# Two 16-head attention layers and the spectral layer between them, run as one pipeline of 16 units

## The reference

```python
x = x + tanh(g_xattn[0]) * one_head_attention(layernorm(x), ctx, mask)       # L0
x = x + tanh(g_ffn[0])   * experts_top_k(layernorm(x)) + shared expert
x = x + tanh(g_xattn[1]) * attention_16_heads(layernorm(x), ctx, bias, mask) # L1
x = x + tanh(g_ffn[1])   * real(ifft(fft(layernorm(x)) @ w)) + bias          # spectral, one 256 x 256 matrix
x = x + tanh(g_xattn[2]) * attention_16_heads(layernorm(x), ctx, mask)       # L2
x = x + tanh(g_ffn[2])   * ternary_mlp(layernorm(x))                         # 256 -> 1024 -> 256
x = x + tanh(g_xattn[3]) * one_head_attention(layernorm(x), ctx)             # L3
x = x + tanh(g_ffn[3])   * experts_top_1(layernorm(x))
```

## Time and profile before

| | us |
|---|---|
| median of 3 runs | 1054.77 (1049.65 to 1055.72) |
| profiled execution, its own time | 1053.23 |
| span of that execution, first to last instruction | 1051.4 |
| TensorE busy | 871.2 (83%) |
| VectorE busy | 445.3 (42%) |
| ScalarE busy | 359.1 (34%) |
| L1, spectral and L2 (from the last product of `spectral_matrix` to the last of L2) | 367.1 to 717.3 |

### The profile page before, as it was taken

The page is one execution under the profiler, slowest core; times in us unless marked ns, Lnnn a source line. Parts: engine busy times, 40 slices in busy tenths (PEclk is TensorE's granted clock), DMA queues, the critical chain, the costliest instruction groups (busy, mean ns, idle before and its releaser), DMA issues. The chain is left out here.

```text
span 1051.4 us, 15194 instructions
## 1 busy us (share of the span) xinstructions
PE 871.2 (83%) x5758; PEld 659.2 (63%) x5758; DVE 445.3 (42%) x1209; ACT 359.1 (34%) x731; POOL 201.4 (19%) x202
## 2 busy tenths in 40 slices
PE   4897999998888968898766799974679788379996
PEld 3774666677777845666554566642456576368885
DVE  1675544301222146654274665534766467400000
ACT  1432222121221225554311455442667543012221
POOL 0127100012344200000010000000345412501222
PEclk8996999998999969999976999996889999589999
DMA  6033600017554370000000000000000000234551
GB/s 202 21 121 121 244 10 11 22 41 264 167 184 118 61 280 1 1 2 2 1 1 0 1 2 1 2 1 1 0 1 1 1 29 34 95 110 157 176 180 18
DMA packets 33871, 70.54 MB, mean 67 GB/s; under 512 B 9219, under 2 KB 23947, under 8 KB 28940
## 3 DMA queue, kind: packets, MB, share of 16 engines
q1 hardware_dynamic: 27081, 60.18, 16.1%
q0 software_dynamic: 6144, 8.31, 4.2%
q10 hardware_dynamic: 578, 1.13, 0.3%
HBM read 54.98 MB, written 14.80 MB: 66 GB/s over the span
## 5 line engine op out<-in xcount | busy, mean ns | idle before, releaser
L1201 ACT ACTIVATE arena<-banks 128x512 f32<-128x512 f32 (+4 forms) x159 | 92.4, 599 | 286.9 <-PE banks L1063 54.9
L592 PE MATMUL banks<-arena 32*128 32x240 f32 (+6 forms) x1808 | 163.9, 381 | 19.2 <-DVE small L1882 14.8
L592 PE MATMUL banks<-ffw,arena 128*128 128x256 f32 (+2 forms) x640 | 126.9, 357 | 15.2 <-DVE x L1976 14.8
L592 PEld LDWEIGHTS banks<-arena 32*128 32x128 f32 (+5 forms) x1808 | 102.8, 165 | 53.1 <-issue 28.8
L592 PEld LDWEIGHTS banks<-ffw,arena 128*128 128x128 f16 (+1 forms) x640 | 87.3, 140 | 47.1 <-issue 23.4
L592 PE MATMUL banks<-arena,ew 128*128 128x256 f32 x512 | 115.1, 384 | 1.4 <-ACT arena L1201 1.4
L592 PE MATMUL banks<-ew,arena 128*128 128x256 f32 x512 | 115.6, 385 | 0.0
L592 PEld LDWEIGHTS banks<-arena,ew 128*128 128x128 f32 x512 | 98.4, 193 | 15.7 <-ACT arena L1201 2.1
L592 PEld LDWEIGHTS banks<-ew,arena 128*128 128x128 f32 x512 | 98.1, 194 | 13.2
L1882 DVE TENSOR_REDUCE small<-banks 128x16 f32<-128x1920 f32 x32 | 69.1, 2158 | 24.2 <-PE banks L592 23.8
L1380 ACT ACTIVATE arena<-banks,mcol 120x2048 f32<-120x2048 f32 x32 | 63.2, 1975 | 23.8 <-PE banks L592 23.8
(11 more groups left out here) (233 smaller groups left out, 1240.7 us busy)
## 6 DMA issues: line engine op xcount, KB each, us to landing
ew<-in_w SPq DMA_DIRECT2D x32, 1024.0 KB
xrow<-arena SPq DMA_DIRECT2D x1, 2064.0 KB, 21.5
arena<-xrow SPq DMA_DIRECT2D x8, 258.0 KB, 4.2
zrow<-arena SPq DMA_DIRECT2D x8, 256.0 KB, 2.2
ffw<-in_shared SPq DMA_DIRECT2D x2, 1024.0 KB, 7.0
acc<-x SPq DMA_DIRECT2D x4, 512.0 KB, 2.9
ffw<-in_tern SPq DMA_DIRECT2D x2, 1024.0 KB
out<-x SPq DMA_DIRECT2D x8, 256.0 KB, 2.0
```

Source lines behind the costliest of these rows:

```text
L592: return pe.matmul(o, l, r, start=a, stop=b)
L1201: return nc.scalar.activation(o, i_, ACT.Copy)
```

## The change

`multi_head(1)`, the spectral rounds and `multi_head(2)` become one function `stream()` on each engine, with units v = 0 to 15: units 0 to 7 are the batches in L1, 8 to 15 the same batches in L2. It runs steps s = 0 to 17. The spectral layer of batch j is put into step j+4, so eight steps (4 to 11, `free` in the code) hold it: on TensorE `spectral_turn(s-4)` takes the place of `turn_z(s+1)`, which moves behind `turned_scores(s-1,0)`; `queries(s+1)` moves behind `scores(s,1)`; `spectral(s-4)` and then `keys(s+1)` come behind `attend(s-1,0)`. The first works in bank 6, the second in bank 7. On ScalarE `take_z` moves behind the first `exps` and `take_back` behind `take_keys`. VectorE gets the spectral layer's statistics and norm one step ahead (steps 3 to 10) and its addition in steps 4 to 11, with buffers of their own (`zS`, `zST`, `veS`, `rstdS`). Three barriers go, those after the experts, L1 and the spectral layer; what is left is numbered anew. In place of the first, VectorE waits for `M_ps`, ScalarE for the experts' last result on VectorE, and SyncE for GpSimd's `later` before it writes the blank rows. The first unit's parts come in another order: keys, values, then the transposed rows and queries.

```diff
@@ SyncE
-            phase_end(sp, 1)
+            sp.wait_ge(su["later"], 7)
             sp.dma_start(xrow[0:T, :].rearrange("(t p) n -> p t n", p=P), bcast(blank, 1, NT)).then_inc(ex["blank"], 16)
@@ GpSimd
+                rstd_of(0)
+                rstd_of(1)
+                for s in range(UN):
+                    if s + 2 < UN:
+                        rstd_of(s + 2)
+                    if 3 <= s < NB + 3:
+                        g.wait_ge(f1["var"], s - 2)
+                        g.tensor_tensor(rstdS, veS, mhalf[:, 0:2], ALU.pow).then_inc(f1["rstd"], 1)
@@ TensorE
-            phase_end(pe, 1)
...
+                def turn_z(v):
+                    pe.wait_ge(q["z"], v + 1)
+                    pe.wait_ge(q["V_sb"], max(v, 1))
+                    if 3 <= v - 2 < NB + 3:
+                        pe.wait_ge(f1["zT_sb"], v - 4)
...
+                def turn_back(v):
...
+                    if 2 <= v < NB + 2:
+                        pe.wait_ge(f1["x"], v - 1)
...
+                def spectral_turn(j):
+                    pe.wait_ge(f1["z"], j + 1)
+                    pe.wait_ge(q["V_sb"], j + 5)
+                    o = psum[6].rearrange("p (k n) -> p k n", k=KC)
+                    for c in range(KC):
+                        for t in range(TB):
+                            m = pe.transpose(o[:, c, t * P:(t + 1) * P], zS[:, t, c * P:(c + 1) * P], ident[:, :])
+                    m.then_inc(f1["zT_ps"], 1)
+
+                def spectral(j):
+                    pe.wait_ge(f1["zT_sb"], j + 1)
+                    pe.wait_ge(q["mT_sb"], j + 4)
+                    for t in range(TB):
+                        for c in range(KC):
+                            m = mm(psum[7][:, t * D:(t + 1) * D], zST[:, c, t * P:(t + 1) * P], Mf[:, c, :],
+                                   c == 0, c == KC - 1)
+                    m.then_inc(f1["y_ps"], 1)
...
-                for part in (turn_z, queries, keys, values):
-                    part(0)
-                for s in range(NB + 2):
+                for part in (keys, values, turn_z):
+                    part(0)
+                queries(0)
+                for s in range(UN + 2):
+                    free = 4 <= s < NB + 4
                     if now:
                         scores(s, 0)
                     if old:
                         turn_max(s - 1)
-                    if new:
+                    if free:
+                        spectral_turn(s - 4)
+                    elif new:
                         turn_z(s + 1)
                     if past:
                         attend(s - 2, 1)
                     if old:
                         turned_scores(s - 1, 0)
-                    if new:
+                    if free:
+                        turn_z(s + 1)
+                    elif new:
                         queries(s + 1)
                     if past:
                         turn_O(s - 2)
                     if now:
                         scores(s, 1)
-                    if new:
+                    if free:
+                        queries(s + 1)
+                    elif new:
                         keys(s + 1)
                     if old:
                         attend(s - 1, 0)
+                    if free:
+                        spectral(s - 4)
+                        keys(s + 1)
                     if past:
                         turn_back(s - 2)
@@ ScalarE
+                act.wait_ge(ex["y_sb"], E)
+                for part in (take_keys, take_z, take_queries):
                     part(0)
...
                     if old:
                         exps(s - 1, 0)
+                    if free:
+                        take_z(s + 1)
                     if new:
                         take_queries(s + 1)
-                    if past:
+                    if past and not free:
                         take_back(s - 2)
                     if new:
                         take_keys(s + 1)
+                    if past and free:
+                        take_back(s - 2)
                     if old:
                         exps(s - 1, 1)
@@ VectorE
+                v.wait_ge(su["M_ps"], 1)
+                V.memset(Vx[:, :, :, HD:], 1.0)
                 take_values(0)
+                v.wait_ge(load["x0"], 32)
+                for n in range(2):
+                    norm_batch(n)
+                    norm_batch_end(n)
+                for s in range(UN + 2):
...
+                    if 3 <= s < NB + 3:
+                        spectral_stats(s - 3)
                     if s >= 2:
                         normalize(s - 2)
-                    if s < NB:
+                    if s < UN:
                         maxima(s, 1)
+                    if 4 <= s < NB + 4:
+                        add_spectral(s - 4)
-                    if s + 2 < NB:
+                    if s + 2 < UN:
                         norm_batch_end(s + 2)
+                    if 3 <= s < NB + 3:
+                        spectral_norm(s - 3)
```

More of the change, by code:

```diff
@@ L979, in keys, with values @@
                     m.then_inc(q["K_ps"], 1)
-                def values(k):
-                    pe.wait_ge(q["K_sb"], k0 + k + 1)
+                def values(v):
+                    L, k = layer(v)
+                    pe.wait_ge(q["K_sb"], v + 1)
                     for c in range(KC):
@@ L1065, in turn_back, with output @@
                     m.then_inc(q["oT_ps"], 1)
-                def output(k):
-                    pe.wait_ge(q["oT_sb"], k0 + k + 1)
+                def output(v):
+                    L, k = layer(v)
+                    pe.wait_ge(q["oT_sb"], v + 1)
                     for t in range(TB):
@@ L1201, in copy @@
                 return nc.scalar.activation(o, i_, ACT.Copy)
-            def take_z(q, i, u, banks=MISC):
-                act.wait_ge(q["zT_ps"], i * 2 + u + 1)
-                copy(zT[:, u], banks[u][:, :].rearrange("p (k n) -> p k n", k=KC)).then_inc(q["zT_sb"], 1)
             def take_weights(a, bank):
@@ L1387, in take_O, with take_back, take_spectral @@
                     copy(OP.rearrange("p g n -> p (g n)"), OW).then_inc(q["O_sb"], 1)
-                def take_back(k):
-                    act.wait_ge(q["oT_ps"], k0 + k + 1)
-                    if k >= 1:
-                        act.wait_ge(q["y_ps"], k0 + k)
+                def take_back(v):
+                    act.wait_ge(q["oT_ps"], v + 1)
+                    if v >= 1:
+                        act.wait_ge(q["y_ps"], v)
                     copy(OT2, psum[7].rearrange("p (k n) -> p k n", k=KC)).then_inc(q["oT_sb"], 1)
-                for part in (take_z, take_queries, take_keys):
+                def take_spectral(j):
+                    act.wait_ge(f1["zT_ps"], j + 1)
+                    copy(zST, psum[6].rearrange("p (k n) -> p k n", k=KC)).then_inc(f1["zT_sb"], 1)
@@ L1396, in multi_head @@
+                act.wait_ge(ex["y_sb"], E)
+                for part in (take_keys, take_z, take_queries):
                     part(0)
-                for s in range(NB + 2):
-                    new, old, past = s + 1 < NB, 1 <= s <= NB, 2 <= s
+                for s in range(UN + 2):
+                    new, old, past = s + 1 < UN, 1 <= s <= UN, 2 <= s
+                    free = 4 <= s < NB + 4
                     if old:
                         take_max(s - 1)
-                    if new:
+                    if free:
+                        take_spectral(s - 4)
+                    elif new:
@@ new lines, in spectral_norm @@
+                def spectral_norm(j):
+                    v.wait_ge(f1["rstd"], j + 1)
+                    if j >= 1:
+                        v.wait_ge(f1["zT_ps"], j)
+                    for t in range(TB):
+                        m = V.tensor_scalar(zS[:, t, :], x[:, 2 * j + t, :], mv[:, 2 + t, 0:1], rstdS[:, t:t + 1],
+                                            ALU.subtract, ALU.mult)
+                    m.then_inc(f1["z"], 1)
+                    v.drain()
+                    xt = x[:, 2 * j:2 * j + 2, :]
+                    V.tensor_tensor(xt, xt, bcast(rows[:, ROWS.index("f1"), :], 1, TB), ALU.add)
```

348 lines of the change are left out of this document (152 added, 196 removed).

## The result

The changed kernel takes 1010.55 us (median of 4 runs, 1007.92 to 1010.74), before 1055.07 in the same comparison; the ratio is 0.957, 95% interval 0.954 to 0.960. A second set of five runs of it gave 1010.51. The forecast was 1009.0, in a range of 999 to 1023.

What follows compares the result with a forecast made beforehand. The prediction took TensorE as busiest (83%), with the loss in filling and emptying the pipeline twice and the serial layer between. 109.28 - 49.1 - 18.0 + 2.0 = 44.2 us off 1053.2 gave 1009.0, range 999 to 1023.

Steps and rivals of the forecast that it cites:

- The seam: Between L1 and L2: 109.28 us go, three more full steps cost 49.1, net 60.2 less before the spectral work.
- The spectral work: Eight free steps: each 2.25 us longer than a full step, 18.6 in all; together 18.0 us more.
- the new wait for the exponentials: TensorE in a free step, before the second scores: stands 0.64 us because the queries no longer cover the exponentials.
- the wait of 0.77 before the values: TensorE in a free step: this wait goes, since ScalarE copies the keys ahead of `take_back`.
- the addition in bank 7: VectorE's spectral addition ahead of `turn_back` in a free step: ends about T+8.8, covered by the keys with 0.2 us spare.
- The start: From the spectral matrix to the first scores: keys and values first bring scores 2.0 us earlier, no clock gain taken.
- The pause before the transposes: TensorE in the start: stands some 3.7 us just ahead of the transposes, 4.65 before.
- Hand-overs bare: Rival: waits for copies in banks 6 and 7 of free steps lose 13 us, giving 1022; chance 0.14.
- Waits filled up: Rival: free steps of 17.26 and full clock at the start, 994 at the least, about 1000 if half; chance 0.10.
- the low bound of 17.26: Free step's length in us if neither the new wait nor the two old ones remained: 14.88 + 2.38.
- Seam: Rival: L1 empties and L2 fills as before, without the spectral stage; 22.1 us at worst, 1031; chance 0.03.
- The clock: Rival: TensorE's clock falls in free steps, 14.2 us more each, 1123 for all eight; chance 0.02.

Runs made afterwards that it cites:

- experiment 3: Changed kernel with ScalarE's old order in the free steps, the copy for the output ahead of the copy of the keys: 1013.78 us, ratio 0.962.
- experiment 4: Changed kernel with VectorE's spectral addition moved behind the two norms, just ahead of the values' addition: 1013.88 us, ratio 0.961.
- experiment 2: Changed kernel with the barrier after the experts put back and the first unit's parts in the old order: 1010.42 us, ratio 0.959.
- the control: The changed kernel run once more, unaltered: 1010.51 us, ratio 0.958.
- experiment 5: Changed kernel with the spectral product ahead of the second scores: 1001.29 us; or in halves, ahead of the first turned and the second scores: 997.03 us.

## Why the prediction was right

**The seam.** Forecast: 109.28 us go, 49.1 come. Measured: three more full steps in 49.10, steps 6 to 9 as long as their neighbours (18.54), so unit 8 waits for nothing that its neighbours don't. The pair without the spectral layer prices seam and start at 28.7 where the rows gave 29.2: 27.2 for the seam (22.1 for emptying and filling, 5.1 for the barrier and the first norms) and 2 for the start.

**The spectral work.** Forecast 18.6 a free step, measured 18.54; 8 x 2.25 = 18.0, measured 148.35 - 8 x 16.37 = 17.4. By its parts: the new wait for the exponentials 0.64, measured 0.60; the wait of 0.77 before the values gone, as ScalarE's order was the reason (experiment 3 brings it back to the hundredth); the addition in bank 7 hidden with 0.2 to spare, measured 0.15, and experiment 4 shows what stands behind that margin; VectorE ready 0.3 ahead of the values, measured 0.29.

**The start.** Forecast 13.84 from the spectral matrix to the first scores, measured 13.66, without the clock's gain, as taken. The pause before the transposes, put at 3.7, was 3.32. In the median the barrier and the start are not to be seen, in the traces they are (experiment 2).

**The sum.** The touched stretch came out 45.9 shorter in the trace, up to the ternary layer's first transposes, against 44.2 up to L2's last output. The difference is 0.6 in the eight steps, 0.2 in the start, 0.2 in steps 0 and 1, some 0.5 in the emptying, whose clock was 0.95 instead of 0.92, and 0.3 behind L2's last output. The part up to the first key product was 4.3 longer in that execution and the part behind 0.9 shorter, so the span shows 42.5: as far below the forecast as the stretch lies above it. In the control, with the same code, steps 0 and 1 alone were 1.4 shorter again. So the terms are right to some tenths each, but that the total of 1009.0 comes within 1.6 of the median is in part luck: the forecast started from an execution 1.8 below the median of before, and parts that it held fixed moved by up to 4.3.

**The rivals.** Hand-overs bare: none was, though experiments 3 and 4 show what each of two choices of order that prevent it is worth: 0.85 and 0.87 us a step. Waits filled up: not by the change, but experiment 5 fills both, so the low bound of 17.26 was attainable, by another order; it was even passed, at 17.10. I had argued that the exponentials stand squarely ahead of the scores; that holds for these scores only, and work that needs neither can go between. Seam: no stall. The clock: 1.00 in all free steps. By the rule of the Trainium skill (TensorE: Matmul & The Clock Gate, "A second HAM failure mode: psum-queue depth-cycling") the more frequent turns through PSUM banks might have made it go up and down; the trace disagrees, with two idle pieces of 0.72 and 0.60 us in 18.54.

What the prediction didn't say: that a third of the gain is clock. It was in the sum, since whole stretches were taken out with the low clock in them (0.81, 0.50, 0.95 in the earlier trace rows), but named as emptying and filling.

## What to carry to other kernels

When independent batches run through several layers, carry the software pipeline across the layers: here the second filling and emptying, with its barrier and the old start, cost 28.7 of 44.5 us, and a short serial layer costs about its TensorE time when it is slipped into the full steps. Walk one full step, each engine with its waits, before choosing where the extra work goes: the same work costs 2.2 us a step in one place and 0.7 in another, and the order of two copies on a half-idle engine is worth 0.8. Read a change of a per cent from the stretch that it touches, cut at the same instructions, and take the same cut from a second execution, since untouched stretches moved by up to 6 us, and two steps just behind the start, with the same code, moved by 2.6.

## What the runs showed that was not expected

The stretch ahead of the change, the same instructions in every kernel, took 361.1 to 366.9 us up to its key row. Between the traces of before and after, TensorE's busy time there differs by 6.9 us (322.04 and 328.91), at a clock of 0.96 and 0.95, and its idle time by 2.4 the other way. Sixteen small products near 15 us took 2.13 us in one and 3.41 in the other. So the same products ran slower in one execution, with no wait that differs as much. The recorded clock doesn't show why: from 15 to 19 us it is 0.99 in the trace of before and 1.00 in that of the changed kernel, where the sixteen take 3.41 and a group of another sixteen, near 18 us, 1.78 instead of 0.99. What sets the pace there was not tried.

Filling a wait of 0.60 us shortened the step by 0.85 (18.54 to 17.69), and both waits of 1.32 by 1.44. The extra is in the products' own time: TensorE is busy 17.22 us in a free step of the changed kernel, 16.97 with the product early and 17.10 with it split. Why is not explained; products of another kind as neighbours, and weight loads that have time to go ahead, would be the place to look.
